# Graph attention on one Trainium2 core: queries kept as three bfloat16 parts, and the weighted sums kept in the same memory

## The chip, the cores and the metric

The kernel runs on one core of one Trainium2 chip. The metric is the device time of one launch in microseconds (us), taken as the median of several runs. Engines are named as the profile names them: PE is TensorE (PEld its weight loads), DVE is VectorE, ACT is ScalarE, POOL is GpSimd, SP is the queue that issues most transfers. A name like L1231 is a line of the kernel before.

## The reference

Two graph layers over 6250 nodes with 256 features and 200,000 edges that are sorted by destination. Only the first layer matters here:

```
h = relu(layernorm(x))
Q, K, V = h@Wq, h@Wk, h@Wv                     # [n, 8 heads, 32]
score = sum(Q[dst]*K[src], last)/sqrt(32) + relu(efeat@W1+b1)@W2 + b2
ex = exp(score - segment_max(score, dst)[dst])
alpha = ex / segment_sum(ex, dst)[dst]
x = x + segment_sum(alpha * V[src], dst) @ Wo + bo
```

The second layer multiplies the new x with 16 relation matrices, gathers one message per edge, weighs it and sums it by destination.

## The kernel before

**Stages.** The program goes through five stages, each ended by a barrier of all engines: tables of the edges (`edge_tables`, to about 103 us of the profiled span), projections of the nodes (`node_projections`, 106 to 264 us), the attention of the edges (`attend`, 264 to 2891 us), the relation messages (`messages`, to about 3700 us), and their sums by destination with the output (`message_sums`, to the end). The change touches the first four. The functions of the change are `edge_tables`, `node_projections` and `attend`; `messages` only reads the sums through another view.

**Steps.** Nodes lie in 49 blocks of 128, edges in 784 groups of 256. A step is a pair (block, group): a step goes to the next group, or, where a group straddles two blocks, stays in the group and goes to the next block. There are 832 steps. Eight steps are a chunk, and the softmax's running maximum is brought up to date once a chunk. One loop body holds 16 steps, written out.

**What a step does in `attend`.** Each engine runs its own list and waits on counters of the others:

- ACT makes `pickT` (`measure`, `pick`), a matrix with a one where an edge's destination is a node of the block, and 11 steps later `onehot`, the same the other way round (`measure_dst`, `hot`).
- PE, in `select` (L1049), multiplies `pickT` by the block's queries and so copies to each of the 256 edges its destination's query: two products of 128x128 by 128x256, all float32, each of which the trace shows as two MATMUL records. `select(s + 1)` waits until DVE has used the products of step s - 1.
- POOL gathers each edge's keys and values from HBM (L911), into 16 slots.
- DVE, in `dot`, multiplies queries and keys (L1138) and sums over each head (L1143). Eleven steps later `weigh` (L1213) multiplies the values by the softmax weights.
- PE, in `add_up` (L1088), multiplies `onehot` by the weighed rows into `sums`, and DVE, in `add` (L1231), adds these to `att` at the block's place. A head's 33rd column carries the sum of the weights.
- Once in eight steps: DVE scans the scores (L1151, L1153), follows the maxima along the chunk (L1169 to L1186, with L1171), and takes the maxima off (L1199 to L1207); `put` (L1193) prepares the next chunk; `rescale` (L1221) multiplies the block's sums. PE has `score`, `up`, `down` and `turn_drop` for these (L1060 to L1079).
- Once in four steps, for as long as groups are left: the edge network on PE (`hidden` L1027, `mlp_out` L1037, `turn_ef` L1020) and ACT. It runs ahead of the steps, and ends near 2715 us; the last 53 steps run without it.

The order of the engines' work within a step is written out by hand (`body`). PE does `select(s + 1)`, the chunk's piece, the network's piece, `add_up(s - 12)`. DVE does `dot(s)`, the chunk's piece, `weigh(s - 11)`, now and then `rescale`, and `add(s - 12)`.

**Projections.** Seven blocks are a batch. DVE normalises a batch (L552, `xn`) while PE works on the batch before; PE turns a block (L636), multiplies it by Wq (L648) and by Wk and Wv (L650); ACT takes the queries out of PSUM, scaled, into `q` (L616) and keys and values into `kvo`, which SP stores. Before block 5 of a batch is taken out, ACT computes the square roots for the next batch; DVE waits for them (L548) and then normalises. POOL fills the weight columns of `kvo` with ones, and then all of `att` with zeros (L534).

**Memory.** `q` holds 49 x 256 float32 for each partition, `att` 49 x 264 float32; both live through `attend`, `att` also through `messages`. Since `att` begins at zero, `add` is a plain sum:

```
to = acc[:, bass.ds(b, 1), :]
nc.vector.tensor_tensor(to, to, sums[u % 2][:, 0:KV - D].unsqueeze(1), ALU.add).then_inc(added, 1)
```

Of the kernel before, what the change touches and what calls it, by code (L numbers as in the profile page):

```python
# [13 lines left out]
F32 = mybir.dt.float32  # L14
BF16 = mybir.dt.bfloat16
I32 = mybir.dt.int32
ALU = mybir.AluOpType
# [49 lines left out]
def build(nc, x, src, dst, edge_attr, edge_type, edge_weight, wq, wk, wv, w1, b1, w2, b2, wo, bo,  # L67
# [11 lines left out]
    with ExitStack() as ctx:  # L79
# [12 lines left out]
        t["ident"] = sb("t_ident", [P, P])  # L92
        t["eps"] = sb("t_eps", [P, 1])
        t["one"] = sb("t_one", [P, 1])
        edge_tables(nc, t, src, dst, edge_type, edge_weight, dstrow_d, pens_d, line_d, src_d, rel_d, norm_d)
        with ExitStack() as att_ctx:
            att = att_ctx.enter_context(nc.sbuf_tensor("att", [P, BLOCKS, H, HD1], F32, side="right"))
            with nc.sbuf_tensor("q", [P, BLOCKS, D], F32) as q:
                node_projections(nc, t, q, att, x, wq, wk, wv, kv_d)
                attend(nc, t, q, att, edge_attr, w1, b1, w2, b2, kv_d, mlp_d, dstrow_d, pens_d, line_d, src_d)  # L100
# [36 lines left out]
def edge_tables(nc, t, src, dst, edge_type, edge_weight, dstrow_d, pens_d, line_d, src_d, rel_d, norm_d):  # L137
# [5 lines left out]
    with ctx:  # L143
# [195 lines left out]
        def _(dve):  # L339
# [50 lines left out]
            nc.vector.tensor_copy(t["block"], blkf[:, :])  # L390
            done(nc.vector.memset(moved[:, 0:1], 0.0))
# [55 lines left out]
def node_projections(nc, t, q, att, x, wq, wk, wv, kv_d):  # L447
# [9 lines left out]
    with ctx:  # L457
# [7 lines left out]
        hT = sb("hT", [P, 3, 2, P])  # L465
        kvo = sb("kvo", [P, B, KV])
# [15 lines left out]
        proj_ready = sem("proj_ready")  # L482
        kv_ready = sem("kv_ready")
# [47 lines left out]
        @block.gpsimd  # L531
        def _(pool):
            pool.memset(kvo[:, :, D:KV], 1.0).then_inc(ones_set, 1)
            pool.memset(att[:, :, :, :], 0.0)  # L534

        @block.vector
        def _(dve):
# [22 lines left out]

            def iteration(i, more):
                for j in range(B):
                    if more:
# [29 lines left out]
            iteration(BATCHES - 2, True)  # L593

        @block.scalar
        def _(act):
# [10 lines left out]
            def iteration(i, more):  # L607
                for j in range(B):
# [4 lines left out]
                    if j == 5 and more:  # L613
                        root(i + 1)
                    act.wait_ge(proj_ready, n + 1)
                    nc.scalar.activation(q[:, bass.ds(n, 1), :].rearrange("p a d -> p (a d)"), qq[s][:, 0:D], ACT.Copy,  # L616
                                         scale=HD ** -0.5)
# [13 lines left out]
        def _(pe):  # L631
# [7 lines left out]
            def iteration(i, more):  # L639
                for j in range(B):  # L640
# [4 lines left out]
                    pe.wait_ge(hT_ready, n + 1)  # L645
                    wait(pe, kv_ready, n + 1 - BACK[j])
# [49 lines left out]
def attend(nc, t, q, att, edge_attr, w1, b1, w2, b2, kv_d, mlp_d, dstrow_d, pens_d, line_d, src_d):  # L696
    ctx, sb, ps, sem = phase(nc)
    RH = R * H
    with ctx:
# [9 lines left out]
        far_node = sb("far_node", [P, 2 * P])  # L709
        pickT = sb("pickT", [P, PICKS, 2 * P])  # L710
# [82 lines left out]
        acc = att[:, :, :, :].rearrange("p b h c -> p b (h c)")  # L793
# [222 lines left out]
        def _(pe):  # L1016
# [26 lines left out]
            def select(s, u):  # L1043
# [4 lines left out]
                for k in range(2):  # L1048
                    last = nc.tensor.matmul(p_q[u % 2][:, k * D:(k + 1) * D], pickT[:, u % PICKS, k * P:(k + 1) * P],  # L1049
                                            q[:, bass.ds(b, 1), :], start=True, stop=True)  # L1050
# [81 lines left out]
        def _(dve):  # L1132
# [82 lines left out]
            def rescale(s, c):  # L1215
# [4 lines left out]
                to = att[:, bass.ds(b, 1), :, :].rearrange("p b h c -> p (b h) c")  # L1220
# [496 lines left out]
```

## Time and profile before

| what | value |
|---|---|
| median of 3 runs | 5838.89 us (5834.64 to 5838.99) |
| the profiled execution | 5842.13 us, its span 5840.2 us |
| busy over the span | PE 87%, PEld 52%, DVE 58%, ACT 57%, POOL 57% |
| mean granted clock of PE | 0.848 of full speed |
| `attend` | about 2627 us of the span |
| `messages` and `message_sums` | about 2950 us of the span |

A busy share is the part of the span in which an engine had an instruction in flight. Over a stage it can be read as a sign of the bound; over the whole span it mixes stages with different limits. The granted clock is 1.00 at 2.4 GHz and 0.50 at 1.2 GHz. Idle time in front of an instruction is shown with what ended it; "issue" means that nothing in the profile did.

### The profile page before, as it was taken

The numbers are of one execution on the slowest core, as the hardware profiler recorded it, in microseconds if no ns is written. First come the engines' busy times: TensorE is split into PE (matmuls) and PEld (weight loads), VectorE is DVE, ScalarE is ACT, GpSimd is POOL, SyncE is SP. The second block draws the span as 40 slices with busy tenths as digits, with TensorE's granted clock in tenths as the row PEclk, the third lists the DMA queues.
The fourth block names the chain that finished last, engine by engine and source line by source line (L and its number), as shares of the span: only waits on it lengthen the run. The fifth ranks groups of instructions, "written<-read, shape, count | busy, mean of one in ns | idle before, by whom it ended". The sixth has DMA issues, their size and how long they took to land. (4 is left out here: it accounts for less than half of the span.)

```text
span 5840.2 us, 108440 instructions
## 1 busy us (share of the span) xinstructions
PE 5074.5 (87%) x22962; PEld 3057.4 (52%) x22963; DVE 3406.7 (58%) x7903; ACT 3349.0 (57%) x8126; POOL 3313.4 (57%) x3407
## 2 busy tenths in 40 slices
PE   5899999999999999999699999776777777777775
PEld 3566666666666666666444444344444444444443
DVE  3289999999999999999733333332333233333323
ACT  1488888888888888887544444333333333333332
POOL 1166666666666666666400000477777777777775
PEclk8999999999999999999899999766566566665665
DMA  2477777777777777777544444433333333333334
GB/s 84 146 215 222 222 221 223 220 224 223 222 221 221 222 223 223 221 222 218 163 133 142 141 141 141 119 105 104 104 104 105 103 104 105 104 104 105 105 103 125
DMA packets 634844, 942.30 MB, mean 161 GB/s; under 512 B 166045, under 2 KB 468255, under 8 KB 634783
## 3 DMA queue, kind: packets, MB, share of 16 engines
q0 software_dynamic: 212992, 661.34, 39.3%
q1 hardware_dynamic: 421790, 280.26, 16.5%
q8 instruction: 24, 0.39, 0.0%
q14 instruction: 38, 0.30, 0.0%
HBM read 808.29 MB, written 132.98 MB: 161 GB/s over the span
## 5 line engine op out<-in xcount | busy, mean ns | idle before, releaser
L911 POOL DMA_INDIRECT kv_rows<-kv_d,idx x1664 | 1667.5, 1002 | 930.3 <-issue 463.3
L1352 PE MATMUL m_sums<-m_rows,m_oh 128*128 128x256 f32 x3328 | 1537.1, 611 | 579.1 <-issue 205.0
L1314 POOL DMA_INDIRECT m_rows<-msg_d,m_idx x1664 | 1594.3, 958 | 537.1 <-issue 377.7
L1352 PEld LDWEIGHTS m_sums<-m_rows,m_oh 128*128 128x128 f32 x3328 | 897.0, 297 | 1219.4 <-issue 687.8
L1664 ACT ACTIVATE m_rows<-m_rows,m_norm 128x256 f32<-128x256 f32 x1664 | 754.2, 500 | 1360.7 <-DMA m_rows<-msg_d,m_idx 1360.7
L1374 DVE TENSOR_TENSOR agg<-agg,m_sums 128x256 f32 x832 | 350.5, 421 | 1452.3 <-PE m_sums L1352 1452.1
L1088 PE MATMUL sums<-kv_rows,onehot 128*128 128x264 f32 x3328 | 932.6, 403 | 10.6 <-DVE kv_rows L1213 3.6
L1049 PE MATMUL p_q<-q,pickT 128*128 x3328 | 868.7, 384 | 13.4 <-ACT pickT L954 9.0
L1088 PEld LDWEIGHTS sums<-kv_rows,onehot 128*128 128x128 f32 x3328 | 573.2, 190 | 385.6 <-issue 313.3
L1635 PE MATMUL p_m<-wr,h1T 128*128 128x512 f32 x1568 | 710.5, 596 | 0.0
L931 ACT ACTIVATE hid<-p_hid,b1s 128x512 f32<-128x512 f32 x784 | 496.3, 684 | 370.5 <-PE p_hid L1027 370.5
L1049 PEld LDWEIGHTS p_q<-q,pickT 128*128 128x128 f32 x3328 | 617.6, 190 | 150.3 <-issue 59.8
L1138 DVE TENSOR_TENSOR prod<-p_q,kv_rows 128x512 f32<-128x512 f32 x832 | 565.7, 680 | 54.5 <-DMA kv_rows<-kv_d,idx 34.8
L1143 DVE TENSOR_REDUCE dots<-prod 128x16 f32<-128x512 f32 x832 | 570.6, 686 | 33.2
L1213 DVE TENSOR_TENSOR kv_rows<-kv_rows,wgt 128x528 f32<-128x528 f32 x832 | 576.2, 693 | 2.7 <-ACT wgt L978 2.7
L961 ACT ACTIVATE far_dst<-t_iota,t_dst 128x128 f32<-128x128 f32 x1664 | 570.3, 393 | 0.5
L1491 POOL TENSOR_TENSOR x_res<-x_res,bos 128x256 f32<-128x256 f32 x49 | 35.5, 726 | 776.3 <-DMA x_res<-in_x_dram 776.3
L1027 PE MATMUL p_hid<-efT,w1s 64*128 64x512 f32 x1568 | 444.5, 644 | 0.7 <-ACT efT L926 0.7
L968 ACT ACTIVATE onehot<-far_dst,t_one 128x256 f32<-128x256 f32 x832 | 417.5, 502 | 47.1 <-PE sums L1088 46.3
L1635 PEld LDWEIGHTS p_m<-wr,h1T 128*128 128x128 f32 x1568 | 287.3, 191 | 285.7 <-issue 283.2
L1231 DVE TENSOR_TENSOR att<-att,sums 128x264 f32 x832 | 351.1, 422 | 145.9 <-PE sums L1088 121.8
L1538 DVE TENSOR_SCALAR msg<-p_m,gate 128x256 f32<-128x256 f32 x392 | 171.7, 479 | 449.3 <-PE p_m L1635 446.7
(180 smaller groups left out, 4455.9 us busy)
## 6 DMA issues: line engine op xcount, KB each, us to landing
msg_d<-msg SPq DMA_DIRECT2D x196, 512.0 KB
dsts<-dstrow_d SPq DMA_DIRECT2D x416, 128.0 KB
ef_raw<-in_edge_attr_dram SPq DMA_DIRECT2D x195, 256.0 KB
kv_rows<-kv_d,idx POOLq DMA_INDIRECT x1664
m_rows<-msg_d,m_idx POOLq DMA_INDIRECT x1664, 2.8
kv_d<-kvo SPq DMA_DIRECT2D x49, 260.0 KB
pens<-pens_d SPq DMA_DIRECT2D x104, 96.2 KB
emlp<-mlp_d SPq DMA_DIRECT2D x104, 64.0 KB
```

Source lines behind the costliest of these rows:

```text
L911: pool.indirect_dma_start(rows[:, u, k, :], None, kv_d[:, :], bass.IndirectOffsetOnAxis(idx[:, half, c:c + 1], 0)).then_inc(gathered[u], 16)
L931: nc.scalar.activation(hid[:, k, :, :], p_hid[k][:, :].rearrange("p (g e) -> p g e", g=U), ACT.Relu, bias=b1s[:, half:half + 1]).then_inc( ...
L961: nc.scalar.activation(far_dst[:, k, :], t["iota"][:, :], ACT.Abs, scale=-1.0, bias=t["dst"][:, bass.ds(2 * s + k, 1)]).then_inc(fard_read ...
L1049: last = nc.tensor.matmul(p_q[u % 2][:, k * D:(k + 1) * D], pickT[:, u % PICKS, k * P:(k + 1) * P], q[:, bass.ds(b, 1), :], start=True, st ...
L1088: last = nc.tensor.matmul(sums[u % 2][:, 0:KV - D], onehot[:, u % HOTS2, k, :], rows[:, u % SLOTS, k, D:KV], start=(k == 0), stop=(k == 1))
L1138: nc.vector.tensor_tensor(prod[:, :, :], p_q[u % 2][:, :].rearrange("p (k d) -> p k d", k=2), rows[:, u, :, 0:D], ALU.mult).then_inc(prod_ ...
L1143: nc.vector.tensor_reduce(dots[:, x, :, u % R, :], prod[:, :, :].rearrange("p k (h c) -> p k h c", h=H), AX.X, ALU.add).then_inc(dots_done, 1)
L1213: nc.vector.tensor_tensor(v, v, wgt[:, x, :, u % R, :].unsqueeze(3).to_broadcast([P, 2, H, HD1]), ALU.mult).then_inc(weighed, 1)
L1314: pool.indirect_dma_start(rows[:, u, k, :], None, table[:, :], bass.IndirectOffsetOnAxis(idx[:, u // 2, c:c + 1], 0)).then_inc(gathered[u] ...
L1352: last = nc.tensor.matmul(sums[u % BANKS][:, 0:width], onehot[:, u % HOTS, k, :], rows[:, u, k, :], start=(k == 0), stop=(k == 1))
L1635: last = nc.tensor.matmul(p_m[c % 4][:, :], hT[:, s, half, :], wr[:, half, 2 * c:2 * c + 2, :], start=(half == 0), stop=(half == 1))
L1664: last = nc.scalar.activation(rows[:, k, :], rows[:, k, :], ACT.Copy, scale=norm[:, bass.ds(2 * s + k, 1)])
```

## The change

**Queries.** The query block is kept as three bfloat16 arrays of 256 columns whose sum is the float32 query. In `node_projections` ACT writes the first part (rounded), DVE subtracts it from the product in PSUM (`split`, into `qr`), rounds the rest into the second part (`second`), and subtracts again for the third (`third`). The three pieces are staggered, one block apart. PE does not use a slot of PSUM again before `split` has read it. In `attend`, `far_node` and `pickT` are bfloat16, and `select` makes three bfloat16 products for each of the two halves, added up in PSUM: six instead of two float32 ones.

**Room.** `q` and `att` share one array, `shelf`, with 50 places of 3 x 256 bfloat16. Block b's queries are at place b + 1, its sums at place b as 264 float32 numbers: where the queries of block b - 1 were. So `att` can't be filled with zeros ahead, but for place 0. Instead `add` multiplies what is there by `keep` of the step, which is 0 on the first step of a block and 1 on others. `keep` is a table made once in `edge_tables`.

```
+            shelf = att_ctx.enter_context(nc.sbuf_tensor("shelf", [P, BLOCKS + 1, 3 * D], BF16, side="right"))
+            q = shelf[:, 1:BLOCKS + 1, :]
+            att = shelf[:, 0:BLOCKS, :].bitcast(F32)[:, :, 0:H * HD1]
...
+            nc.vector.memset(t["keep"][:, 0:1], 0.0)
+            nc.vector.tensor_tensor(t["keep"][:, 1:TSTEPS], nbase[:, 1:TSTEPS], nbase[:, 0:TSTEPS - 1], ALU.is_equal)
...
-            pool.memset(att[:, :, :, :], 0.0)
+            pool.memset(att[:, 0, :], 0.0)
...
+            def q_part(part, n):
+                return q[:, bass.ds(n, 1), part * D:(part + 1) * D].rearrange("p a d -> p (a d)")
+
+            def split(i, j):
+                n = B * i + j
+                first = isinstance(i, int) and i == 0
+                dve.wait_ge(q0_ready, n + 1)
+                nc.vector.scalar_tensor_tensor(out=qr[:, j, :], in0=qq[SLOT[j]][:, 0:D], scalar=HD ** -0.5, in1=q_part(0, n),
+                                               op0=ALU.mult, op1=ALU.subtract).then_inc(qr_ready, 1)
+                if not (first and j < 1):
+                    second(n - 1, (j - 1) % B)
+                if not (first and j < 2):
+                    third(n - 2, (j - 2) % B)
+
+            def second(n, j):
+                dve.wait_ge(qr_ready, n + 1)
+                nc.vector.tensor_copy(q_part(1, n), qr[:, j, :]).then_inc(q1_ready, 1)
+
+            def third(n, j):
+                dve.wait_ge(q1_ready, n + 1)
+                nc.vector.tensor_tensor(q_part(2, n), qr[:, j, :], q_part(1, n), ALU.subtract)
+
             def iteration(i, more):
                 for j in range(B):
+                    split(i, j)
                     if more:
...
+            iteration(BATCHES - 1, False)
+            second(BLOCKS - 1, B - 1)
+            third(BLOCKS - 2, B - 2)
+            third(BLOCKS - 1, B - 1)
...
-                    nc.scalar.activation(q[:, bass.ds(n, 1), :].rearrange("p a d -> p (a d)"), qq[s][:, 0:D], ACT.Copy,
-                                         scale=HD ** -0.5)
+                    nc.scalar.activation(q[:, bass.ds(n, 1), 0:D].rearrange("p a d -> p (a d)"), qq[s][:, 0:D], ACT.Copy,
+                                         scale=HD ** -0.5).then_inc(q0_ready, 1)
...
+                    wait(pe, qr_ready, n + 1 - BACK[j])
                     wait(pe, kv_ready, n + 1 - BACK[j])
...
-        far_node = sb("far_node", [P, 2 * P])
-        pickT = sb("pickT", [P, PICKS, 2 * P])
+        far_node = sb("far_node", [P, 2 * P], BF16)
+        pickT = sb("pickT", [P, PICKS, 2 * P], BF16)
...
-                    last = nc.tensor.matmul(p_q[u % 2][:, k * D:(k + 1) * D], pickT[:, u % PICKS, k * P:(k + 1) * P],
-                                            q[:, bass.ds(b, 1), :], start=True, stop=True)
+                    for part in range(3):
+                        last = nc.tensor.matmul(p_q[u % 2][:, k * D:(k + 1) * D], pickT[:, u % PICKS, k * P:(k + 1) * P],
+                                                q[:, bass.ds(b, 1), part * D:(part + 1) * D].rearrange("p b d -> p (b d)"),
+                                                start=(part == 0), stop=(part == 2))
...
-                to = acc[:, bass.ds(b, 1), :]
-                nc.vector.tensor_tensor(to, to, sums[u % 2][:, 0:KV - D].unsqueeze(1), ALU.add).then_inc(added, 1)
+                to = att[:, bass.ds(b, 1), :].rearrange("p b e -> p (b e)")
+                nc.vector.scalar_tensor_tensor(out=to, in0=to, scalar=t["keep"][:, bass.ds(s, 1)], in1=sums[u % 2][:, 0:KV - D],
+                                               op0=ALU.mult, op1=ALU.add).then_inc(added, 1)
```

The views of `att` in `rescale` and in `normalise` of `messages` are written for the new shape and otherwise the same.

## Rows read from the trace of the kernel before

**Rows 1.** Busy time by stretch of `attend`, with and without the edge network.

```profile
core 0: us, PE busy (x) PEld busy (x) DVE busy (x) ACT busy (x) POOL busy (x), PEclk, DMA share, GB/s
300.00:2700.00 2400.00, 2393.25 (x15933) 1562.19 (x15933) 2193.32 (x4789) 2036.67 (x5174) 1535.96 (x1535) 1.00 0.78 222
2720.00:2860.00 140.00, 117.93 (x467) 73.33 (x466) 135.28 (x299) 92.02 (x253) 98.81 (x97) 1.00 0.76 215
```

**Rows 2.** Line L1138, one a step, in two stretches: min/median/max ns, first and last start.

```profile
L1138 DVE TENSOR_TENSOR prod<-p_q,kv_rows x736: 672/682/687, 401.4 to 2697.7; 128x512 f32<-128x512 f32 x184
...
L1138 DVE TENSOR_TENSOR prod<-p_q,kv_rows x48: 671/678/685, 2722.6 to 2860.3; 128x512 f32<-128x512 f32 x48
```

**Rows 3.** DVE groups by shape, 300 to 2700 us: busy us, mean ns | idle before them.

```profile
L1231 DVE TENSOR_TENSOR att<-att,sums 128x264 f32 x761 | 321.3, 422 | 140.5 <-PE sums L1088 118.0 <-issue 22.1 <-DVE att L1221 0.2
...
L1204 DVE SCALAR_TENSOR_TENSOR top<-pens,ends,top 64x256 f32<-64x256 bf16 x96 | 45.8, 477 | 3.4
...
L1207 DVE TENSOR_TENSOR fwd<-p_soft,top 64x256 f32<-64x256 f32 x96 | 39.9, 416 | 3.3
```

**Rows 4.** The same view, 2720 to 2860 us, without the edge network.

```profile
L1231 DVE TENSOR_TENSOR att<-att,sums 128x264 f32 x47 | 19.7, 418 | 1.2 <-issue 1.2
```

**Rows 5.** PE in order of time: start us, us, work (a run's last record included).

```profile
1503.36 1.03 PE L1049 MATMUL p_q<-q,pickT 128*128 x4
1504.23 1.05 PE L1088 MATMUL sums<-kv_rows,onehot 128*128 128x264 f32 x4
...
1514.98 0.66 PE L1020 MATMUL p_hid<-t_ident,ef_raw 128*128 128x128 f32 x4
1515.47 1.06 PE L1088 MATMUL sums<-kv_rows,onehot 128*128 128x264 f32 x4
1516.36 1.03 PE L1049 MATMUL p_q<-q,pickT 128*128 x4
1517.32 0.45 PE L1079 MATMUL p_soft<-t_ident,fwd 64*128 64x64 f32 x2
```

**Rows 6.** In order of time: a chunk's first PE matmul, DVE's two late adds.

```profile
1506.10 0.62 PE L1060 MATMUL p_soft<-t_ident,dots 128*64 128x128 f32 x4
...
1525.68 0.43 DVE L1231 TENSOR_TENSOR att<-att,sums 128x264 f32 x1 [0.73 <-PE sums L1088]
...
1528.59 0.43 DVE L1231 TENSOR_TENSOR att<-att,sums 128x264 f32 x1 [0.55 <-PE sums L1088]
```

**Rows 7.** Weight loads and matmuls at known and unknown clocks, in time; last the stretch's clock.

```profile
24.53 0.15 PEld L279 LDWEIGHTS count<-passed,ones 128*128 128x128 bf16 x1 [0.20 <-issue]
24.88 0.15 PEld L279 LDWEIGHTS count<-passed,ones 128*128 128x128 bf16 x1 [0.20 <-issue]
...
L279 PE MATMUL count<-passed,ones x6: 507/555/555, 23.9 to 25.6; 128*128 128x418 bf16 x6
...
123.14 0.34 PEld L650 LDWEIGHTS kv<-w_qkv,hT 128*128 128x128 f32 x1 [0.52 <-issue]
123.99 0.34 PEld L650 LDWEIGHTS kv<-w_qkv,hT 128*128 128x128 f32 x1 [0.52 <-issue]
...
L648 PE MATMUL qq<-w_qkv,hT x4: 634/634/793, 120.4 to 121.9; 128*128 128x256 f32 x4
...
119.30:124.90 5.60, 5.55 (x12) 3.24 (x13) 1.77 (x6) 0.77 (x2) 0.00 (x0) 0.50 0.42 131
```

**Rows 8.** Projections in order of time: PE, ACT and DVE in one batch.

```profile
150.56 0.38 PE L636 MATMUL xT<-t_ident,xn 128*128 128x128 f32 x2
...
150.85 0.38 ACT L616 ACTIVATE q<-qq 128x256 f32 x1 [1.59 <-PE kv L650]
...
157.88 0.20 DVE L548 RECIPROCAL rstd<-std 128x7 f32<-128x7 f32 x1 [3.68 <-ACT std L599]
```

**Rows 9.** The stage's first normalise and POOL's fill, and one table operation.

```profile
L552 DVE TENSOR_SCALAR xn<-xin,mv,rstd x7: 394/400/2920, 116.2 to 120.7; 128x256 f32<-128x256 f32 x7
...
108.11 10.88 POOL L534 MEMSET att<- 128x12936 f32 x1
...
37.66 1.02 DVE L392 TENSOR_TENSOR moved<-grpf 1x835 f32<-1x835 f32 x1
```

More of the change, by code:

```diff
@@ L92, in build @@
         t["ident"] = sb("t_ident", [P, P])
+        t["keep"] = sb("t_keep", [P, TSTEPS])
         t["eps"] = sb("t_eps", [P, 1])
@@ L96, in build @@
         with ExitStack() as att_ctx:
[L97 to L100, printed above, removed]
+            shelf = att_ctx.enter_context(nc.sbuf_tensor("shelf", [P, BLOCKS + 1, 3 * D], BF16, side="right"))
+            q = shelf[:, 1:BLOCKS + 1, :]
+            att = shelf[:, 0:BLOCKS, :].bitcast(F32)[:, :, 0:H * HD1]
+            node_projections(nc, t, q, att, x, wq, wk, wv, kv_d)
+            attend(nc, t, q, att, edge_attr, w1, b1, w2, b2, kv_d, mlp_d, dstrow_d, pens_d, line_d, src_d)
             with nc.sbuf_tensor("x1", [P, BLOCKS, D], F32) as x1:
@@ L465, in node_projections @@
         hT = sb("hT", [P, 3, 2, P])
+        qr = sb("qr", [P, B, D])
         kvo = sb("kvo", [P, B, KV])
@@ L482, in node_projections @@
         proj_ready = sem("proj_ready")
+        q0_ready = sem("q0_ready")
+        qr_ready = sem("qr_ready")
+        q1_ready = sem("q1_ready")
         kv_ready = sem("kv_ready")
@@ L792, in attend @@
         block = ctx.enter_context(nc.Block())
-        acc = att[:, :, :, :].rearrange("p b h c -> p b (h c)")
         chunks = edge_attr[0:FULL_GROUPS * GE, :].rearrange("(g p k) f -> p g (k f)", p=P, k=2)
@@ L1219, in rescale @@
                     dve.wait_ge(added, s)
-                to = att[:, bass.ds(b, 1), :, :].rearrange("p b h c -> p (b h) c")
+                to = att[:, bass.ds(b, 1), :].rearrange("p b (h c) -> p (b h) c", h=H)
                 nc.vector.tensor_tensor(to, to, scale[:, :].unsqueeze(2).to_broadcast([P, H, HD1]), ALU.mult).then_inc(scaled, 1)
@@ L1507, in normalise @@
             def normalise(b, s, n):
-                a = att[:, bass.ds(b, 1), :, :].rearrange("p b h c -> p (b h) c")
+                a = att[:, bass.ds(b, 1), :].rearrange("p b (h c) -> p (b h) c", h=H)
                 nc.vector.tensor_scalar(den[:, :, :], a[:, :, HD:HD1], 1.0e-30, None, ALU.max).then_inc(den_link, 1)
```

## The prediction

> **What bounds the kernel now.** I read the page for the stages, then busy time by stretch. From 300 to 2700 us PE is busy for all but 7 of 2400 us, at full clock, DVE for 91% [rows 1]. Next I asked for the pace: L1138 comes once a step, 736 times from 401.4 to 2697.7 us, so 2296.3/735 = 3.124 us a step [rows 2]. Then who waits: DVE's only large idle time in these 2400 us is 140.5 us in front of L1231, nearly all for `add_up` on PE, or 140.5/768 = 0.18 us a step [rows 3]. So PE sets the pace, and DVE needs 3.124 - 0.18 = 2.94 us of it. The last 53 steps show this without arithmetic: the edge network has ended, PE is at 84%, DVE at 97% with 1.2 us of waits at L1231 [rows 1, 4], and the pace is (2860.3 - 2722.6)/47 = 2.930 us [rows 2]. The reader is to see two engines 6% apart: whatever is taken from PE beyond that share is not gained.
>
> **PE's part in `attend`.** Start to start, `select` is 4 records in 0.87 us (1503.36 to 1504.23) and `add_up` 0.89 us (1515.47 to 1516.36) [rows 5]. The new `select` has six bfloat16 products. The trace has bfloat16 products in L279 alone: 418 columns every 0.35 us, or 0.84 ns a column [rows 7]. Which clock is that? The clock has no record so early. Two marks say half speed: a record there lasts 0.555 us, 0.20 over its spacing, and in a stretch at a granted 0.50 L648 lasts 0.634 us with a spacing of 0.43 (half of L650's 0.85, which has twice the columns), again 0.20 over; at full clock the four L1049 records end 1.03 us after the first start, so the last lasts 1.03 - 3 x 0.22 = 0.37, only 0.15 over its spacing [rows 5, 7]. The other mark is the rate: the float32 records take 0.85/512 = 1.66 ns a column at half clock, twice L279's. So at full clock 256 bfloat16 columns should take 256 x 0.42 = 0.107 us. Each needs a weight load of 128 columns; L1020, which loads 128 and streams 128 columns four times, takes 0.49 us for four (1514.98 to 1515.47), so such a load fits in 0.12 us at most [rows 5]. I take 0.11 us for each product, 0.66 us for `select`, 0.21 us less a step. Bounds: 0.107 us, and 0.21 us if L279 ran at full clock already.
>
> The Trainium skill (TensorE: Matmul & The Clock Gate, Back-to-back issue gap) gives N/2.4 + 2.5 ns for a warm product, 109 ns here. Its LDWEIGHTS section gives P/1.2, 107 ns for 128 columns, so by it each load would just hide and the sum stay as it is; no row here shows a bfloat16 load at a granted clock of 1.00.
>
> **DVE's part in `attend`.** L1231 becomes an operation with a scalar for each partition. The trace has this kind in L1204, 256 columns in 477 ns, against 416 ns for the plain one of the same size, L1207 [rows 3]: 61 ns, 63 with the eight columns more. It falls on the engine that is then the bound, so nothing hides it. Bounds: 0, since L1204 differs in reading no PSUM, and 0.08. The moving address of `keep` adds a register operation in DVE's queue, which usually runs ahead of the engine; on one add in eight, behind the chain of small operations, it does not, and I charge 0.09/8 = 0.01 us a step. ACT writes bfloat16 instead of float32 at no cost: it is busy for 85% [rows 1], and waits on PE. POOL's gathers have room too (64%).
>
> **Who is last then.** DVE: 2.930 + 0.063 + 0.011 = 3.004. PE: 3.124 - 0.21 = 2.91. Does DVE still wait at the two adds where it does now? Anchor on a chunk's first matmul, L1060 at 1506.10. The later add starts at 1528.59, 22.49 us on; with six shorter selects PE gets there 6 x 0.21 = 1.26 us earlier, at 1527.33. DVE, rid of both waits (0.73 and 0.55) and with seven scalars to pay (0.44), wants it at 1527.75. That leaves 0.4 us in 25, and 0.7 at the earlier add [rows 6]. So no wait on average, but little margin: I add 0.01 us and take 3.014 us a step. From about step 12 on there are 767 steps with the edge network: 767 x (3.124 - 3.014) = -84.4 us. The 53 without it get slower: 53 x 0.074 = +3.9 us.
>
> **Projections.** `split`, `second` and `third` are 49 x 3 operations on DVE, which mostly waits in this stage: the square roots alone are waited for 3.68 us in a batch [rows 8]. The work itself is hidden; its order is not: at block 5 of each batch `split` now stands in front of the next batch's normalisation, and it waits for PE's product of block 5, after which PE wants the normalised rows. What is late: ACT takes the product at 150.85, 0.29 us after PE was free for the next turn at 150.56, and needs 0.38 [rows 8]; then three DVE operations, each at most L1207's 0.42 less an overlap of 0.08 with the next, 1.02 in all [rows 3]; the reciprocal 0.20 with 0.04 of gap [rows 8]; one normalise 0.40 [rows 9]. Sum: PE stands 2.3 us, for six batches +14.0 us. Bounds: 1.5 us (the three DVE operations at 0.08 less each, and the reciprocal's gap and part of ACT's take hidden) and 4 us (PE's clock falls in some of the gaps).
>
> At the stage's start there is a gain that the diff hides. The first normalise took 2.92 us instead of 0.40, and ended as POOL's fill of `att` (108.11 + 10.88 = 118.99) did; PE's first turn waits for it [rows 9]. The fill of one block is over long before: -2.5 us. Bounds: -2.6 and 0, if something else then releases PE. The Trainium skill (SBUF — State Buffer, the shared port pair) has DVE and GpSimd exclude each other on one pair of ports for a whole instruction; the 2.92 us row agrees.
>
> **Tables.** `keep` is one operation of 835 columns like L392, 1.02 us, with a tiny fill, on DVE's chain ahead of what PE waits for: +1.1 us [rows 9]. `messages` reads the same columns through another view: nothing.
>
> **Sum.** -84.4 + 3.9 + 14.0 - 2.5 + 1.1 = -67.9 us. The profiled execution took 5842.1 us, so 5774.2; it lies 3.2 us over the median of 5838.9, and the forecast for the median is 5771 us, 1.2% less. A change within 0.2% (12 us) cannot be told from none.
>
> **Rivals.**
>
> *DVE pays little for its scalar.* Then DVE wants 2.94 and PE 2.91, and they get in each other's way: about 2.96 us a step, 767 x 0.164 = 126 us off `attend`, some 5730 us. For it: L1204 and L1207 differ in more than the scalar. Against it: 61 ns is too much for two types. Chance 0.10.
>
> *PE pays for changing between bfloat16 and float32.* PE does pay for a change of the tile's shape: L1049 to L1079, 128 rows to 64, is 0.96 us where L1049 to L1088 is 0.87 [rows 5]. If a change of type costs 0.09 too, twice a step, 0.18 of the 0.21 us is gone, the pace is 3.09 to 3.12 and only 0 to 25 us come back against 16 us of additions: about 5830, from 5815 to 5855. Against it: L1020, a transpose of another mode but the same shape, goes over to L1088 free of charge [rows 5]. Chance 0.10. The same time would come out if the queue of PE, with a register operation for each part's address, fed the products at 0.14 us.
>
> *The other side: bfloat16 products don't run at 0.11 us.* The place is `select`, the price 0.21 us each if L279 ran at full clock. Then `select` takes 1.28 us, 0.41 more than now, and `attend` grows by 767 x 0.41 = 314 us, to about 6165 us. It decides from 0.14 us on: at (3.124 - 2.26)/6, with 2.26 us of PE's other work, the pace is as before and the additions alone make it slower. For it: the view of stretches gives 1.00 where no record exists, and the weight loads of L279 last 0.15 us, longer than 0.11 [rows 7]. Against it: the two marks above, and L1020's spacing. Chance 0.06.
>
> *The gain is given back by coupling.* `select(s + 1)` waits for DVE's product of step s - 1, and `add_up` for `weigh`; with 0.4 us of margin, waits could leave 0.03 to 0.06 us a step: 5795 to 5820. Chance 0.14, inside the range.
>
> The forecast as described has the remaining 0.60.
>
> **Range and chances.** 5735 to 5820 us: from the cheap scalar to the coupling; outside are the slow products, most of the change of type, and a little on the low side. Faster by over 0.2%: 0.60 + 0.10 + 0.14, and a third of the type rival, 0.86 in all. Within 0.2%: 0.05. Slower: the slow products and the rest of the type rival, 0.09.
>
> **What the profile after would show.** Right: L1138's spacing near 3.01 us with and without the edge network alike; L1231 near 485 ns, with hardly any idle time before it; `select` 0.66 us start to start; PE's idle time now in front of matmuls, released by DVE; a gap of 2.3 us on PE at each batch of the projections; the first normalise at 0.4 us. Wrong, if L1231 keeps waiting for L1088, if `select` takes 0.8 us or more, if L1231 stays at 422 ns, or if PE's clock falls within `attend`.

## The result, and the profile of the changed kernel

The changed kernel takes 5820.11 us (median of 10 runs, 5817.15 to 5828.27); the kernel before took 5835.74 us in the same comparison (10 runs, 5833.25 to 5838.99). The ratio is 0.9973, with a 95% interval of 0.9965 to 0.9982: 15.6 us or 0.27% faster, where 1.2% was predicted. 5820.11 lies at the very end of the range, 0.1 us outside.

Busy time by stretch of `attend`, the same stretches as in [rows 1]:

```profile
core 0: us, PE busy (x) PEld busy (x) DVE busy (x) ACT busy (x) POOL busy (x), PEclk, DMA share, GB/s
300.00:2700.00 2400.00, 2306.58 (x17724) 1434.36 (x17725) 2258.44 (x4837) 2059.89 (x5238) 1601.92 (x1556) 1.00 0.79 225
```

PE now has 93 us of idle time in 2400 instead of 7; DVE is at 94%. No engine is full. The line that comes once a step, min/median/max ns and first and last start, answers to [rows 2]:

```profile
L1176 DVE TENSOR_TENSOR prod<-p_q,kv_rows x747: 671/683/687, 401.1 to 2696.0; 128x512 f32<-128x512 f32 x187
...
L1176 DVE TENSOR_TENSOR prod<-p_q,kv_rows x41: 672/676/685, 2716.1 to 2835.4; 128x512 f32<-128x512 f32 x41
```

With the edge network a step takes 2294.9/746 = 3.076 us (3.074 over whole chunks of eight steps; predicted 3.014). Without it, it takes 119.3/40 = 2.983 us (predicted 3.004). DVE's groups and PE's `select`, 300 to 2700 us, mean ns and the idle time before them, answer to [rows 3]; the last is the weight loads of `select`:

```profile
L1086 PE MATMUL p_q<-shelf,pickT 128*128 x4680 | 646.7, 274 | 5.8 <-DVE prod L1176 0.3
...
L1269 DVE SCALAR_TENSOR_TENSOR shelf<-shelf,t_keep,sums 128x264 f32 x767 | 370.1, 483 | 61.3 <-PE sums L1126 28.1 <-issue 20.6 <-DVE shelf L1259 0.2
...
L1086 PEld LDWEIGHTS p_q<-shelf,pickT 128*128 128x128 bf16 x4680 | 441.0, 98 | 214.7 <-issue 81.4
```

The add costs 483 ns instead of 422, as predicted, and its row still has waits for PE. One wait is new, that of PE for DVE once in a chunk; before, it occurred only behind the end of the edge network. The second line is DVE's wait for PE (us in all, times, longest):

```profile
PE p_soft L1117 <- DVE fwd L1245: 38.6, 94, 0.9
DVE shelf L1269 <- PE sums L1126: 28.1, 102, 0.3
```

Where the 22.3 us between the two profiled spans (5840.2 and 5817.9) are, by the first and last instruction of each stage:

| part of the span | before | after | difference | predicted |
|---|---|---|---|---|
| start of the span to the first product of `attend` | 273.6 | 292.1 | +18.5 | +12.6 |
| `attend`, to its last weighted sum | 2616.4 | 2584.2 | -32.2 | -80.5 |
| `messages`, `message_sums` | 2950.2 | 2941.6 | -8.6 | 0 |

The last line is in neither the change nor its theory. The profiled execution of before lay 6.4 us above its median, that of after 0.4 below, which may be a part of it; the medians differ by 15.6, not 22.3 us. Five more traces of kernels whose last two stages are those of the changed one (e6, e12, e16, e17, e18, below) have 2940.5 to 2946.7 us there. So the same code varies by 6 us, and the one trace of before lies 3.6 us above the highest; whether anything but chance is in it is not shown.

**The middle of a chunk.** PE and DVE in order of time (start us, us), as in [rows 5, 6]:

```profile
1517.06 0.82 PE L1086 MATMUL p_q<-shelf,pickT 128*128 x6
...
1517.73 0.41 DVE L1245 TENSOR_TENSOR fwd<-p_soft,top 64x256 f32<-64x256 f32 x1
...
1518.30 0.42 PE L1117 MATMUL p_soft<-t_ident,fwd 64*128 64x64 f32 x2 [0.42 <-DVE fwd L1245]
...
1518.87 1.13 PE L1126 MATMUL sums<-kv_rows,onehot 128*128 128x264 f32 x4 [0.15 <-issue]
1519.09 0.68 DVE L1176 TENSOR_TENSOR prod<-p_q,kv_rows 128x512 f32<-128x512 f32 x1
...
1520.03 0.86 PE L1086 MATMUL p_q<-shelf,pickT 128*128 x6
...
1526.24 0.82 PE L1086 MATMUL p_q<-shelf,pickT 128*128 x6
...
1526.99 0.64 PE L1073 MATMUL p_mlp<-hid,w2s 128*32 128x128 f32 x16
...
1528.06 1.06 PE L1126 MATMUL sums<-kv_rows,onehot 128*128 128x264 f32 x4
...
1528.95 0.82 PE L1086 MATMUL p_q<-shelf,pickT 128*128 x6
...
1529.28 0.49 DVE L1269 SCALAR_TENSOR_TENSOR shelf<-shelf,t_keep,sums 128x264 f32 x1 [0.28 <-PE sums L1126]
1529.62 0.71 PE L1126 MATMUL sums<-kv_rows,onehot 128*128 128x264 f32 x2
```

Read it from the top. `select` is 0.67 us start to start (1528.95 to 1529.62), and 0.75 with the change of the tile's shape behind it (1526.24 to 1526.99). PE comes to `turn_drop` (L1117) 0.42 us too early and stands until DVE's L1245 has ended at 1518.14. The next `select` may not overwrite its half of PSUM before DVE's product at 1519.09 has read it: that ends at 1519.77, PE starts at 1520.03. Then come the steps in which PE has network pieces as well, and 9.25 us later it is DVE that waits for PE, 0.28 us at the add of 1529.28. So neither engine is last all the time: DVE sets the middle of a chunk, PE sets its end.

**What the waits cost.** By steps of the chunk, averaged over 95 chunks of this trace, the add of the seventh step starts 0.28 us after the instruction before it has ended, that of the sixth 0.14 us (in the trace of before 0.55 and 0.73). Where these two adds don't wait (e16 below), they start 0.08 us before the instruction ahead of them has ended, so a wait also costs this overlap, and the loss is 0.28 + 0.08 + 0.14 + 0.08 = 0.58 us a chunk, 0.073 a step. That is the distance from 3.00 to 3.074. The row of L1269 shows half of it (28.1 us of some 56): it counts neither the lost overlap nor the waits of 0.14.

**Batch ends of the projections.** PE, ACT and DVE at the end of one batch, and the granted clock (third number from the end) of the block behind the gap and of the blocks behind that:

```profile
159.05 0.38 ACT L652 ACTIVATE shelf<-qq 128x256 f32 x1 [1.41 <-PE kv L687]
...
159.59 0.42 DVE L577 SCALAR_TENSOR_TENSOR qr<-qq,shelf 128x256 f32<-128x256 f32 x1 [1.84 <-ACT shelf L652]
...
159.94 0.28 DVE L586 CAST shelf<-qr 128x256 f32 x1
160.13 0.42 DVE L590 TENSOR_TENSOR shelf<-qr,shelf 128x256 f32 x1
160.47 0.20 DVE L556 RECIPROCAL rstd<-std 128x7 f32<-128x7 f32 x1
160.70 1.06 DVE L560 TENSOR_SCALAR xn<-xin,mv,rstd 128x256 f32<-128x256 f32 x3
161.17 0.44 PE L672 MATMUL xT<-t_ident,xn 128*128 128x128 f32 x2 [2.25 <-DVE xn L560]
...
165.66 0.45 PE L672 MATMUL xT<-t_ident,xn 128*128 128x128 f32 x2
```

```profile
161.40:165.60 4.20, 4.20 (x10) 1.97 (x9) 0.36 (x2) 0.38 (x1) 0.00 (x0) 0.62 0.07 27
165.70:174.00 8.30, 8.30 (x31) 5.10 (x30) 4.17 (x13) 3.63 (x12) 0.00 (x0) 0.99 0.52 173
```

The chain is the predicted one and so is its length. A block takes 2.80 us; at the six batch ends it takes 5.22, 5.22, 5.21, 5.22, 5.09 and 4.99, together 14.15 us more (predicted 14.0). But in four of the six cases the block behind the gap took 4.37 to 4.55 us instead of 2.80 as well, since PE's granted clock fell to 0.62 in that stretch: another 6.7 us. The other two blocks behind a gap took 2.86. The prediction had named the fall as a bound and left it out of the sum. One term went the other way and was in no sum: PE's first block of the stage took 4.95 us instead of 6.07, since the granted clock rose sooner (0.81 over 120.5 to 122.9 us, where before had 0.54 over 121.8 to 125.3). In the other traces of this stage it took 4.8 to 6.2 us, so these 1.1 us are no effect of the change.

**The stage's start.** The first normalise, POOL's fill and `keep`, answering to [rows 9]:

```profile
109.03 0.32 POOL L542 MEMSET shelf<- 128x264 f32 x1
...
117.95 1.09 PE L672 MATMUL xT<-t_ident,xn 128*128 128x128 f32 x4 [43.06 <-DVE xn L560]
```

```profile
L394 DVE TENSOR_TENSOR t_keep<-nbase 128x835 f32<-128x835 f32 x1 | 1.0, 1011 | 0.0
```

All normalises of this stage last 404 to 415 ns. The first starts at 117.39 instead of 116.22 (+1.17; 1.1 was predicted for `keep`), and PE's first turn at 117.95 instead of 119.28: -1.33 = 1.17 - 2.5. The 2.5 us is a difference within each trace. The match of the 1.17 is partly luck: `keep` itself takes 1.01 us, but in e6, e12, e16, e17 and e18 the first normalise starts anywhere from 116.6 to 117.8.

### The profile page after: what moved, and what is told of

Same layout as the page of the kernel before. It is cut to its first block and busy times, and to the rows that moved or that the text cites. A ratio compares the mean times of both kernels' runs of the same rounds, so it can differ in the third digit from the quotient of the medians.

```text
span 5817.9 us, 113702 instructions
## 1 busy us (share of the span) xinstructions
PE 4956.4 (85%) x24626; PEld 2902.3 (50%) x24627; DVE 3495.7 (60%) x8052; ACT 3345.4 (58%) x8126; POOL 3342.8 (57%) x3407
## 5 line engine op out<-in xcount | busy, mean ns | idle before, releaser
L947 POOL DMA_INDIRECT kv_rows<-kv_d,idx x1664 | 1715.4, 1031 | 848.6 <-issue 450.2
L1086 PE MATMUL p_q<-shelf,pickT 128*128 x4992 | 692.1, 274 | 20.9 <-ACT pickT L990 9.1
L1086 PEld LDWEIGHTS p_q<-shelf,pickT 128*128 128x128 bf16 x4992 | 467.8, 98 | 254.8 <-issue 115.8
L1269 DVE SCALAR_TENSOR_TENSOR shelf<-shelf,t_keep,sums 128x264 f32 x832 | 401.3, 482 | 65.1 <-PE sums L1126 30.4
```

The source lines that it names most:

```text
L947: pool.indirect_dma_start(rows[:, u, k, :], None, kv_d[:, :], bass.IndirectOffsetOnAxis(idx[:, half, c:c + 1], 0)).then_inc(gathered[u], 16)
```

## The experiments

All start from the changed kernel, but e5. They ran on several chips, and in e1 to e5, e7 to e11 and e13 to e15 the kernel before, run beside them, took 6609 to 6722 us, 13 to 15% more than here. There, a time stands only beside that of the kernel before, and a pace only beside another that was run together with it. The record gives two chip numbers, 1 and 3, to runs of both kinds (e5 and e16, e10 and e6), so whether the chip makes the difference is open. Experiments on the pace that fell there were run again, but for two: the turn moved alone (e2, e7) and the plain add (e4, e9) have no run beside which 3.074 can be put.

**e1: the batch end of the projections.** DVE normalises the next batch first and splits the queries of blocks 5 and 6 behind it.

```
                 for j in range(B):
-                    split(i, j)
+                    if j < 5 or not more:
+                        split(i, j)
...
+                    if j >= 5 and more:
+                        split(i, j)
```

> The changed kernel with one edit: in blocks 5 and 6 of a batch DVE normalises the next batch before it splits the queries. Theory (the order on DVE makes PE stand): PE's gap of about 3.3 us at each of the six batch ends goes, and the projections end 17 to 20 us earlier than in the changed kernel, some 5800 us in all. Rival (the stage is longer because DVE has more work, or PE waits for the splits before it may use a slot of PSUM again): the gaps stay or move, and under 8 us come back. The pace of the attention stays at 3.074 us a step under both.

Measured: 6786.4 us (before beside it 6714.7). The last keys and values of the stage were taken out at 259.4 us, 20.0 us earlier than in the changed kernel (279.4), and the first product of `attend` came at 271.9 instead of 292.1. PE's blocks take 2.80 us throughout, but for the stage's first. So the 21 us at the batch ends are an effect of DVE's order alone; the work of `split` is hidden, and behind the stage's first block no block is longer than 2.80 us, so the clock did not fall where there was no gap.

**e5: the fill, on the kernel before.** POOL waits for the first batch's normalisation before it fills `att`.

```
+            pool.wait_ge(xn_ready, B)
             pool.memset(att[:, :, :, :], 0.0)
```

> The kernel before with one edit: POOL fills att with zeros only after the first batch is normalised, not at the start of the projections. Theory (POOL's fill holds up DVE's first normalise): that operation takes 0.4 us instead of 2.92, PE's first turn comes 2.5 us earlier relative to the stage's start, and the projections end 2.5 us earlier. Rival (the first normalise is slow for another reason, such as the landing of the weights or code): it stays at 2.9 us. A second possibility: the fill then holds up some later operation of DVE by as much, which costs nothing if DVE has room there.

Measured: 6717.0 us against 6721.6. The fill now starts at 119.02, and the first normalises take

```profile
L553 DVE TENSOR_SCALAR xn<-xin,mv,rstd x7: 404/406/411, 116.6 to 118.6; 128x256 f32<-128x256 f32 x7
```

instead of 2920 ns for the first [rows 9]: the fill was what held it up.

**e2, e3, e4 and e7, e8, e9, e11: the pace, where only runs made together can be compared.** Three edits, each alone. The first turns the edge features of a quad one step later on PE:

```
-                    if u % U == 2 and is_quad(m + 2):
-                        turn_ef(m + 2)
...
                         select(s + 1, u + 1)
+                    if u % U == 3 and is_quad(m + 2):
+                        turn_ef(m + 2)
```

> The changed kernel with one edit: PE's four transposes of edge features stand one step later, in steps 3 and 7 of a chunk in place of 2 and 6, ahead of turn_drop. Theory (PE is held by DVE at step 3 and then has more work in steps 4 to 6 than DVE): 0.44 us leave the piece in which PE is late, and fill time in which PE stands; DVE's wait at the add of step 6 goes, that at step 5 stays; the pace falls from 3.074 to 3.03 to 3.04 us a step, 25 to 35 us less. Rival (DVE itself takes 3.07 us a step while the edge network runs, from memory traffic or its queue): no change, 3.07. Second rival (ACT becomes late because it gets the features later): 3.08 or more.

> [...] The run with both edits of order gave 5776.5 us in all. Theory: the pace falls from 3.074 to 3.03 to 3.04 us, the projections stay as long as in the changed kernel: about 5793 us. Rival (the pace depends on DVE and not on where PE's work stands): 3.07.

Measured: 6696.9 us against 6714.7, and 6646.9 against 6609.6. The second multiplies one of the three parts of a query:

```
-                    for part in range(3):
+                    for part in range(1):
```

> The changed kernel with only the first of the three parts of a query multiplied: two products a step instead of six, 0.44 us less work for PE. It leaves out the second and third part, so the queries are rounded to bfloat16. Theory (waits for PE at two adds of a chunk are all that keeps DVE from its own pace): 3.00 us a step, with and without the edge network, and no idle time of DVE at the add but what follows the rescale. Rival (DVE's own pace is 3.07 while the network runs): 3.07 stays. Rival 2 (PE is the bound throughout): the pace would fall by far more, to 2.7.

> [...] Theory: 3.00 us a step with and without the edge network. Rival (DVE's own pace is 3.07 while the network runs): 3.07. Rival (PE is the bound throughout): 2.7.

> [...] Theory: 3.00 us a step with and without the edge network. Rival (DVE's own pace is 3.07 while the network runs): 3.07. Rival (PE is the bound throughout): 2.7.

Measured: 6756.6 against 6714.7, 6681.1 against 6609.6, 6757.1 against 6693.0. The third adds plainly, without `keep`:

```
-                nc.vector.scalar_tensor_tensor(out=to, in0=to, scalar=t["keep"][:, bass.ds(s, 1)], in1=sums[u % 2][:, 0:KV - D],
-                                               op0=ALU.mult, op1=ALU.add).then_inc(added, 1)
+                nc.vector.tensor_tensor(to, to, sums[u % 2][:, 0:KV - D], ALU.add).then_inc(added, 1)
```

> The changed kernel with the plain add of the kernel before in place of the one with the scalar. It leaves out the clearing of a block's sums, and takes the sum of weights as at least 1. Theory (DVE sets the pace from step 7 to 3 of a chunk, PE from 4 to 6): only the five or six adds on DVE's piece give back their 63 ns: 3.074 - 0.04 = 3.03 to 3.04 us a step, and DVE's waits at the adds of steps 5 and 6 get longer; 2.93 without the edge network. Rival (DVE sets the pace throughout): 3.074 - 0.074 = 3.00. Rival (PE does): 3.07 stays.

> [...] Theory (DVE sets the pace on one piece of the chunk and PE on the other): 3.03 to 3.04 us a step, 2.93 without the network. Rival (DVE throughout): 3.00. Rival (PE throughout): 3.07.

Measured: 6858.7 against 6714.7, 6758.1 against 6609.6. These don't say what a piece is worth at a pace of 3.074. But e1 to e4 ran together, and in `attend` e1 is the changed kernel. The product's spacing was 3.78 us in e1, 3.63 in e2, 3.71 in e3 and 3.83 in e4 (one run each): the moved turn brought 0.15 us a step, twice what the missing four products brought, and the plain add, less work for DVE, came out slower. e7, e8 and e9 came in the same order, 3.60, 3.64 and 3.74. Why the plain add is the slowest no run here shows, and its forecast of 3.03 to 3.04 stays untested. e1 also shows that the changed kernel itself was over 1% slower there than the kernel before, even without its gaps at the batch ends.

**e6 and e18: both orders changed.** e1 and e2 in one kernel; all the work is kept.

> The changed kernel with both edits of order: DVE normalises before it splits in blocks 5 and 6 of a batch, and PE's four transposes stand one step later, ahead of turn_drop. [...] Theory: the projections end 18 to 20 us earlier than in the changed kernel, and the pace goes from 3.074 to 3.03 to 3.04 us; together 45 to 55 us less than the changed kernel, so 5765 to 5775 us. Rival (DVE takes 3.07 us a step by itself while the edge network runs): only the 18 to 20 us, 5800 us.

Measured: 5776.5 us, before beside it 5835.5. The pace in `attend` is 3.045, the stage of the projections ends at 258.5. The same kernel again:

> The changed kernel with the batch-end normalisations ahead of the split and TensorE's turn of edge features one step later, all work kept, for an interval. It gave 5776.5 us in one look on one chip (pace 3.045) and 1.0015 of the kernel before on a chip where the engines' own queue instructions took long. If the first is what the order is worth: ratio 0.989 to 0.991 at a pace of 3.04 to 3.05.

Measured: 5777.73 us (4 runs, 5773.87 to 5780.04), before 5835.02; ratio 0.9901, 95% interval 0.9884 to 0.9917. L1179, the product in this kernel:

```profile
L1179 DVE TENSOR_TENSOR prod<-p_q,kv_rows x723: 671/683/686, 402.0 to 2599.2; 128x512 f32<-128x512 f32 x181
```

2197.2/722 = 3.043 us. Against the changed kernel's trace 21.2 us come from the start (first product at 270.9) and 21.0 us from `attend` (2563.2 instead of 2584.2); the medians differ by 42.4. The wait at the add of the chunk's seventh step is gone, that of the sixth is still 0.15 us. The kernel with the turn alone moved was never run at this speed, so the two halves are told apart by stage and not by a run. This is the fastest version that computes everything.

**e10 and e12: PE takes the network last.** With e1's edit, PE does `add_up` ahead of the step's network pieces:

```
+                    if is_step(s - LATE - 1):
+                        add_up(s - LATE - 1, u - LATE - 1)
                     if is_quad(m + 1):
                         if u % U == 0:
                             hidden(m + 1, 0)
...
-                    if is_step(s - LATE - 1):
-                        add_up(s - LATE - 1, u - LATE - 1)
```

> The changed kernel with DVE normalising before it splits, and with PE's pieces of the edge network moved behind add_up in each step (as much work as before, in another order). With the transposes alone moved, the pace was 3.045 us, DVE still waited at the add of step 5, and a small wait came up at the scans. Theory (the order on PE, not the amount of its work, keeps DVE from its own pace): no wait of DVE at the adds of steps 5 and 6, 3.00 to 3.02 us a step, 5745 to 5760 us in all. Rival (PE's pieces of the network then reach ACT too late and PE waits for hid): 3.05 or more. Rival (DVE has 3.05 to 3.07 of its own): no change.

> Second run of the kernel with both orders changed and PE's network pieces behind add_up. The first met a chip where the queues' own instructions took 0.7 us in stretches, also in the kernel before (6693 us). Theory: no wait of DVE at the adds of steps 5 and 6, 3.00 to 3.02 us a step, 5745 to 5760 us in all. Rival (ACT gets the network's pieces too late): 3.05 or more. Rival (DVE has 3.05 to 3.07 of its own): no change.

Measured: e10 6926.0 us against 6693.0 (ratio 1.035); e12 6451.85 against 5844.16, ratio 1.104 (1.102 to 1.106), a pace of 3.915. My expectation failed, and the chunk shows why:

```profile
1501.09 1.13 PE L1066 MATMUL p_hid<-efT,w1s 64*128 64x512 f32 x4
...
1502.27 1.27 ACT L970 ACTIVATE hid<-p_hid,b1s 128x512 f32<-128x512 f32 x2 [1.91 <-PE p_hid L1066]
...
1503.82 0.50 ACT L1007 ACTIVATE onehot<-far_dst,t_one 128x256 f32<-128x256 f32 x1
...
1504.38 1.16 PE L1129 MATMUL sums<-kv_rows,onehot 128*128 128x264 f32 x4 [1.01 <-ACT onehot L1007]
```

ACT's list has `take_hidden` ahead of `hot`. With PE's `hidden` behind `add_up`, ACT waits for PE's network, makes `onehot` only then, and PE's next `add_up` waits for that. An edit on one queue made a ring with the order of another.

**e13 and e16: ACT's order with it.** As e12, and ACT does `pick` and `hot` ahead of `take_hidden`, `take_mlp` and `take_ef`.

> The edit: the batch-end normalisations go ahead of the split, TensorE takes a step's pieces of the network (hidden, output, turned features) behind that step's weighted sum instead of ahead of it, and ScalarE takes their results behind that step's selection and destination matrices instead of ahead of them. Nothing is left out. Theory (VectorE waits in the add at two of eight steps because network pieces stand ahead of the weighted sum, and the ring of waits between TensorE and ScalarE in the run before came from ScalarE's order alone): the pace of `attend` falls to 3.00 to 3.02 us, the waits of L1269's row on TensorE nearly go, the whole takes 5745 to 5765 us. Rival (the order is right only where TensorE has room, and it has none at 3.05): the pace stays 3.04 to 3.08. Rival (the ring is TensorE's own): above 3.3 us a step.

> The run before once more, on another chip, because the chip before spent time in the engines' own queue instructions and hid the pace. TensorE takes a step's network pieces behind that step's weighted sum, ScalarE takes their results behind that step's selection and destination matrices; all work is kept. Theory (VectorE's waits in the add come from TensorE's order): pace of `attend` 3.00 to 3.02 us, the whole 5745 to 5765 us. Rival (no room left on TensorE): 3.04 to 3.08. Rival (the ring of waits is TensorE's own): above 3.3 us a step.

Measured: e13 6715.3 us against 6609.0; e16, on another chip, 5791.1 against 5841.7. The product of e16, and the waits of DVE's lines from 1000 to 2000 us:

```profile
L1179 DVE TENSOR_TENSOR prod<-p_q,kv_rows x717: 672/684/693, 402.1 to 2598.9; 128x512 f32<-128x512 f32 x180
```

```profile
DVE fwd L1192 <- issue: 10.1, 40, 0.3
DVE shelf L1272 <- issue: 8.9, 41, 0.2
DVE prod L1179 <- issue: 2.5, 14, 0.2
DVE prod L1179 <- PE p_q L1089: 1.2, 7, 0.2
```

The ring is gone: ACT's order alone had made 3.915. But the pace is 2196.8/716 = 3.068, not the 3.00 to 3.02 of my theory. DVE's adds don't wait for PE any more, as it said; instead the first scan of a chunk (L1192) stands for 0.25 us on average. The view names no releaser for it; by the order of the work it should be PE's `score`, which now stands behind more work, but that is not shown. The rival "no room left on TensorE" (3.04 to 3.08) held. With this much work on PE, moving a piece moves the wait: beside the 3.007 of e17 below, e6 lost 0.04 us a step, e16 0.06, the changed kernel 0.07.

**e14: the same kernel as e18, where the kernel before too took longer.**

> The changed kernel with the batch-end normalisations ahead of the split and TensorE's turn of edge features one step later. Nothing is left out. It gave 5776.5 us in one look. If that holds: ratio to the kernel before 0.988 to 0.992.

Measured: 6614.76 us against 6609.01, ratio 1.0015 (1.0005 to 1.0026). From 1000 to 2000 us the instructions of DVE, PE and ACT last as long as in e18 (the add 484 ns against 482, the product 682 against 681), and the waits between engines have grown: those of the add for PE, first in e14, then in e18, are

```profile
DVE shelf L1272 <- PE sums L1129: 77.6, 68, 1.5
```

```profile
DVE shelf L1272 <- PE sums L1129: 3.0, 19, 0.2
```

One more thing differs, on the queues. Their register operations take 0.08 us at most from 1000 to 2000 us in all traces of the faster group. In every trace of the slower one some of them take 0.2 to 1.0 us, 57 to 96 times in these 1000 us and mostly on SP. One line of SP, first in e14, then in e18 (min/median/max ns):

```profile
L864 SPq MOVE dsts<-dstrow_d x140: 16/36/787, 1003.9 to 1999.7; - x140
```

```profile
L864 SPq MOVE dsts<-dstrow_d x164: 29/32/39, 1003.3 to 1994.4; - x164
```

The transfers themselves are not longer: a packet of 4160 bytes of the gather has a median of 161 ns in every trace. Whether the long queue operations cause the longer waits is not shown. The ratios 0.9901 and 1.0015 are both to the kernel before, so they say what the whole change with both orders is worth, 1% in one place and nothing in the other. What the order alone is worth they don't say; e1 beside e2 shows that the moved turn helped there too.

**e15 and e17: less work for PE.** As e3: four of the six products of a `select` are left out, so PE has 0.44 us less to do in a step and DVE all of its own.

> Of the three parts of a query only the first is multiplied: two of TensorE's six passes of a selection remain, so the queries are coarser. TensorE's work falls by 0.44 us a step, VectorE's stays. Theory (the 0.06 us a step above the forecast are waits for TensorE): pace 2.99 to 3.01 us as in the tail, the whole 5765 to 5785 us. Rival (they are VectorE's own, or from contention with the gathers while the network runs): pace 3.05 to 3.08, the whole above 5805 us.

> Once more, on another chip: of the three parts of a query only the first is multiplied, so the queries are coarser. TensorE's work falls by four products a step (0.44 us), VectorE's stays. Theory (the 0.06 us a step above the forecast are waits for TensorE): pace 2.99 to 3.01 us as in the tail, the whole 5765 to 5785 us. Rival (they are VectorE's own, or come from the network's other work beside it): pace 3.05 to 3.08, the whole above 5805 us.

Measured: e15 6659.9 us against 6609.0; e17 5776.8 against 5848.0, and this is the run that decides (one execution):

```profile
L1176 DVE TENSOR_TENSOR prod<-p_q,kv_rows x764: 671/683/686, 401.7 to 2695.9; 128x512 f32<-128x512 f32 x191
```

2294.2/763 = 3.007 us a step, with the edge network and the gathers at work. DVE's order and its instructions are those of the changed kernel (the add 482 ns), and the waits of the add for PE have gone from 28.1 to 6.3 us:

```profile
L1269 DVE SCALAR_TENSOR_TENSOR shelf<-shelf,t_keep,sums 128x264 f32 x783 | 377.0, 482 | 26.5 <-issue 19.9 <-PE sums L1126 6.3 <-DVE shelf L1259 0.2
```

So DVE's own need is 3.00 to 3.01 us, as predicted, and the 0.07 us above it are waits for PE.

## Why the prediction was wrong

The direction and nearly every price were right; the size was a quarter of the forecast. What failed is a step between the prices.

1. **The failed step: "Who is last then", the anchor.** I followed PE from a chunk's first matmul (L1060 at 1506.10) over 22.5 us to the late add and credited it with six shorter `select`s, 1.26 us. That holds only if PE is never held up on the way, as in the trace of before. In the changed kernel DVE holds it up in the middle: `turn_drop` waits for DVE's L1245, and the next `select` for its product. What PE saved ahead of that point brought nothing, it stood for 0.42 us there, and from `turn_drop` on only three `select`s count. Before, from `turn_drop` at 1517.32 [rows 5] to the late add at 1528.59 [rows 6], it was 11.27 us; less 3 x 0.21 that is 10.64, and DVE needs 10.98 - 0.28 - 0.08 - 0.14 - 0.08 = 10.4 for the same way. So PE was last by 0.2 us even on paper; it took 10.98, the 0.34 more being PE's later start of the next `select`, which waited for DVE. The margin of 0.4 us was in truth a shortfall of 0.58 us a chunk. The margin was also too large by its own rows: it took off DVE's two waits (0.73 and 0.55) and not the two overlaps of 0.08 that come back with them. That the 0.58 us is waiting for PE is shown by e17, and e6 and e18 show that PE's order moves it; that it is the standing at `turn_drop` which wastes the first three `select`s is read from the one trace, and no run takes it away by itself. In the sum: -84.4 came out as 767 x 0.050 = -38. `attend` as a whole gained 32.2 us, since the first 16 steps took 2.0 us more than before and the end behind the last product 1.1.
2. **The rival that held.** "The gain is given back by coupling" had the mechanism, the size (0.03 to 0.06 us a step; measured 0.06 over the forecast) and nearly the time (5795 to 5820), and a chance of 0.14. The time fits partly by luck: the start took 5.9 us more than forecast, and the last two stages 8.6 less for no reason known. A margin of 0.4 us in 25, with two waits for each other in every step, had called for more.
3. **`select`.** Six bfloat16 products at 0.11 us: 0.67 us start to start, predicted 0.66. The "slow products" rival is dead; so is the change of type, since `select` to `add_up` is 0.67 with no surcharge, and only the change of shape costs 0.08, about what it did before (0.96 - 0.87 [rows 5]). That rival's range was also wrong in its low end: by its own terms, 0 to 25 us back against 16, it begins at 5830, not 5815.
4. **The add.** Predicted +61 to 63 ns, measured 483 - 422 = 61. The cheap scalar is dead. Without the edge network the pace went from 2.930 to 2.983, 0.02 less than the 0.074 predicted: 53 x 0.053 = +2.8 us, predicted +3.9. Half of that is the queue's register operation, for whose 0.09 us the prediction names no row: it cost 0.002 us a step, not 0.011, as the add behind `rescale` waits 0.217 us instead of 0.204. The other 0.01 is open.
5. **Projections.** The gaps are 14.15 us, predicted 14.0. The clock's fall behind four of them, 6.7 us, was kept as a bound (4 us a batch end in all) and not in the sum, where the stage's total is 21.2 us. e1 confirms both: without the gaps the whole 20 us come back.
6. **Start.** -2.5 us for the fill and +1.1 for `keep` measured -2.5 and +1.17; e5 confirms the first, and the second is within what the start varies by.

What stays open is the 8.6 us of the last two stages, and why the gain of the change vanishes where the waits between engines are longer.

## What to carry to other kernels

- When two engines wait for each other within each step, don't compare their sums over a period. Find the last point at which one holds up the other, start there, and credit only the savings between it and the next wait; savings ahead of it can be lost, as here.
- With margins of some per cent, a faster engine gives back much of its gain through its order. Moving a piece that no one waits for urgently (here the turn of the edge features, one step later) brought 21 of the 48 us that `attend` was short of the forecast; but look first at the lists of the other engines, since the same kind of move made a ring and cost 0.9 us a step.
- A step inserted at a hand-over between two engines costs its latency, however idle the inserting engine is, and the gap can cost a second time through the clock.

## What the runs showed of the hardware

- Identical instructions, identical lengths, 13 to 15% more time: in one group of runs the waits between engines were longer and single register operations of the queues took up to 1.0 us (e14 beside e18), and there the whole change, with both orders, was worth nothing (1.0015) instead of 1% (0.9901).
- Six gaps of 2.0 to 2.25 us on PE: in four of them the granted clock over the next block was 0.57 to 0.62, in the other two 1.00, as behind the gap of 2.03 us at 139.09:

```profile
139.40:143.80 4.40, 4.40 (x18) 2.80 (x17) 1.52 (x6) 1.60 (x5) 0.00 (x0) 1.00 0.05 18
185.20:189.60 4.40, 4.40 (x12) 2.15 (x11) 0.33 (x2) 0.38 (x1) 0.00 (x0) 0.62 0.06 22
```

  The Trainium skill (TensorE: Matmul & The Clock Gate, What's actually happening) says that what the gate looks at runs on its own time, so that the same kernel can come out one way or the other; the two rows agree. So do other traces of the same stage: of the same six gaps, four were followed by a fall in e17, but not the same four (the one at 161.22 was not, the block behind it took 2.86 us), and all six in e2 (0.60 to 0.61 over the next 4.4 us).
- DVE's instructions can overlap by 0.08 us where nothing holds them (above, L590 lasts from 160.13 to 160.55, and the reciprocal starts at 160.47), so a wait can cost 0.08 us more than the idle time shown in front of it.
